# Attention with experts on one core: in the late steps three of 64 score tiles are exponentiated on VectorE, and expert rows are added six row tiles at a time

## The reference

```python
q = heads(x @ Wq.T); k = heads(x @ Wk.T); v = heads(x @ Wv.T)      # 16 heads of 8 columns
q = q * cos + _rotate_half_interleaved(q) * sin                    # k likewise
attn = jnp.einsum('bhnd,bhmd->bhnm', q, k) * scale
attn = jax.nn.softmax(attn, axis=-1)
out = jnp.einsum('bhnm,bhmd->bhnd', attn, v)
...
gate_weights = jax.nn.softmax(x @ gate_w + gate_b, axis=-1)
topk_vals, topk_idx = jax.lax.top_k(gate_weights, 2)               # 2 of 8 experts a row
h = gelu(x w1 + b1); h = gelu(h w2 + b2); expert_out = h w3 + b3
return jnp.sum(topk_vals[..., None] * gathered, axis=2)
```

## Time and profile before

| | us |
|---|---|
| three runs | 640.11, 642.52, 643.66 |
| median | 642.52 |
| the profiled execution | 641.5 |
| its span, first to last instruction | 639.8 |

### The profile page before, as it was taken

The page is one execution under the profiler, slowest core; times in us unless marked ns, Lnnn a source line. Parts: engine busy times, 40 slices in busy tenths (PEclk is TensorE's granted clock), DMA queues, the critical chain, the costliest instruction groups (busy, mean ns, idle before and its releaser), DMA issues.

```text
span 639.8 us, 12291 instructions
## 1 busy us (share of the span) xinstructions
PE 599.6 (94%) x4152; PEld 260.1 (41%) x4152; DVE 239.1 (37%) x742; ACT 546.8 (85%) x555; POOL 166.9 (26%) x187
## 2 busy tenths in 40 slices
PE   9889999999999998998999999999898998999895
PEld 6323332222222222222999999982222222222221
DVE  5655224766352335022565556630202020211204
ACT  3799999999999998999555555569999999999994
POOL 2700000001444444531122221223332333323310
PEclk9999999999999999999999999999999999999999
DMA  7654611532464246783333333311212111121204
GB/s 226 182 181 163 233 34 50 198 138 99 149 210 149 91 140 227 246 260 82 81 76 74 74 74 74 74 37 42 71 44 69 58 58 57 62 77 42 71 13 135
DMA packets 82625, 70.74 MB, mean 111 GB/s; under 512 B 44288, under 2 KB 58400, under 8 KB 82576
## 3 DMA queue, kind: packets, MB, share of 16 engines
q1 hardware_dynamic: 76000, 56.34, 29.1%
q0 software_dynamic: 5856, 13.05, 6.6%
q10 hardware_dynamic: 720, 0.71, 0.5%
HBM read 32.92 MB, written 32.96 MB: 103 GB/s over the span
## 4 chain that ended last, share of the span: by engine, by line
PE 62%; ACT 17%; issue 12%; DMA 3%; DVE 3%; SPq 1%; POOL 1%; DVEq 1%; ACTq 0%; POOLq 0%
PE ps L1411 18%; ACT probs L663 15%; PE ps L1394 11%; PE ps L1343 10%; PE ps L1335 5%; PE ps L1356 5%; PE ps L1318 3%; PE ps L1262 2%; ACT probs L641 2%; DMA k_st<-k_d 2%; DMA work<-slots_y_d,slot_i 2%; PE ps L1298 2%; PE ps L1225 1%; PE ps L1196 1%; DVE x_all L1133 1%
## 5 line engine op out<-in xcount | busy, mean ns | idle before, releaser
L663 ACT ACTIVATE probs<-ps 128x1536 f32<-128x1536 f32 (+1 forms) x308 | 408.6, 1432 | 8.2 <-PE ps L1394 6.6
L1411 PE MATMUL ps<-probs,v_st 128*32 128x512 f32 x1792 | 238.7, 604 | 4.4 <-DVE v_st L789 3.2
L1394 PE MATMUL ps<-q_st,k_st 32*128 32x512 f32 x896 | 154.5, 494 | 22.4 <-ACT probs L663 18.3
L1394 PEld LDWEIGHTS ps<-q_st,k_st 32*128 32x128 f32 x896 | 57.9, 181 | 235.0 <-ACT probs L663 172.7
L677 ACT ACTIVATE work<-ps,work 128x256 f32<-128x256 f32 (+1 forms) x156 | 64.9, 455 | 60.4 <-PE ps L1343 60.2
L541 POOL DMA_INDIRECT slots_x_d<-xn_all,slot_i x64 | 62.9, 983 | 196.9 <-DVE expert_i L987 127.2
L579 POOL DMA_INDIRECT work<-slots_y_d,slot_i x64 | 60.6, 947 | 122.0 <-PE ps L1411 79.2
L1343 PE MATMUL ps<-work 128*128 128x256 f32 (+1 forms) x312 | 68.0, 361 | 0.0
L641 ACT ACTIVATE probs<-ps 128x1024 f32<-128x1024 f32 x64 | 60.6, 1034 | 3.7 <-PE ps L1298 2.7
L1411 PEld LDWEIGHTS ps<-probs,v_st 128*32 128x32 f32 x1792 | 35.6, 107 | 60.7 <-issue 54.5
L789 DVE COPY v_st<-v_all 128x128 f32<-128x128 f32 (+1 forms) x32 | 8.5, 265 | 131.3 <-PE ps L1411 131.3
(11 more groups left out here) (177 smaller groups left out, 379.0 us busy)
## 6 DMA issues: line engine op xcount, KB each, us to landing
k_d<-parts SPq DMA_DIRECT2D x8, 1024.0 KB, 5.7
q_d<-parts SPq DMA_DIRECT2D x8, 1024.0 KB
q_st<-q_d SPq DMA_DIRECT2D x30, 256.0 KB
k_st<-k_d SPq DMA_DIRECT2D x30, 256.0 KB
slots_x_d<-parts SPq DMA_DIRECT2D x5, 1024.0 KB, 7.4
work<-slots_x_d SPq DMA_DIRECT2D x128, 32.0 KB, 1.9
slots_y_d<-work POOLq DMA_DIRECT2D x32, 128.0 KB, 2.2
work<-work SPq DMA_DIRECT2D x24, 128.0 KB
```

The source lines that it names most:

```text
L663: nc.scalar.activation(group_probs(phase, g)[:, 0:size, :], group_slot(g)[:, 0:size * HALF].rearrange("p (h n) -> p h n", n=HALF), ACT.Exp ...
L1394: ins = nc.tensor.matmul(group_slot(g)[:, n * HALF:(n + 1) * HALF], k_st[32 * h:32 * h + ROWS, mt * P:(mt + 1) * P], q_st[32 * h:32 * h + ...
L1411: ins = nc.tensor.matmul(o_ps[32 * h:32 * h + 32, :], v_window(mt, h, half), group_probs(phase, half * HALF_GROUPS + g)[:, n, :], start=be ...
```

## The change

In the late steps the 64 tiles of a step are dealt out anew (LATE_ITEMS). 60 go to ScalarE as 20 groups of three that run on across the two halves of the queries. The other four are one block, the second half of the queries with the first tile of keys. Their scores go one after another into aux_ps (help_scores, iterations 2 to 5). For heads 0, 3 and 2 VectorE reads them, scaled, into SBUF (read_help), and computes the exponential of all three at once, 1536 columns, by eight instructions (help_exps): split off the nearest power of two by adding a large constant, shift that into the exponent, evaluate a polynomial of fifth degree on the rest, multiply. Head 1 stays in aux_ps and is exponentiated by ScalarE after its group 7. The polynomial is not scaled to a leading coefficient of one; the factor that it lacks is put on ScalarE's exponentials too, as a bias of 6.62 (exp_bias), and falls out in the division. TensorE multiplies the helped block in iteration 17 (help_values). The turn of the last step's result moves from iteration 5 to 9, since aux_ps is in use before. A step has two groups fewer and is written as a loop of one step on TensorE and ScalarE; VectorE's late steps are written out.

Gathers are for six row tiles a step (GATHER = 6), in six steps instead of seven, paced by every second block, and added a step later, between the three readings of aux_ps. finish_rows for the first three batches moves to steps 11, 12 and 13. Steps before 9 are as before.

```diff
-GATHER = 5
+GATHER = 6
...
+LATE_ITEMS = [(0, mt, h) for mt in range(MT) for h in range(HG)] + [(1, mt, h) for mt in range(1, MT) for h in range(HG)]
+LATE_GROUPS = len(LATE_ITEMS) // 3
+LATE_BLOCKS = [(0, mt) for mt in range(MT)] + [(1, mt) for mt in range(1, MT)]
+HELP_AT = 2
+HELP_HEADS = (0, 3, 2, 1)
+HELP_VALUES = 17
+EXP_COEFFS = (-7.287735462188721, 41.80864715576172, -180.93753051757812, 522.0867309570312, -753.2122192382812)
+EXP_SHIFT = 6.62434696468868
+EXP_MAGIC = 1.5 * 2 ** 23 + 127 + 256
...
+        he_s, he_t, he_g, he_p = (part(2 * GATHER * C + 3 * HALF * k, 3 * HALF) for k in range(4))
...
+        help_probs = probs[:, PROB_RING - 1]
...
+                sp.wait_ge(S["scores_done"], group_units(t) + (LATE_ITEMS.index((0, MT - 1, HG - 1)) // 3 + 1))
                 load_half(q_st, q_d, t + 1, 0, S["q0_loaded"])
-                sp.wait_ge(S["scores_done"], group_units(t) + KEYS_READ)
+                sp.wait_ge(S["scores_done"], group_units(t) + (LATE_ITEMS.index((1, MT // 2 - 1, HG - 1)) // 3 + 1))
                 load_half(k_st, k_d, t + 1, 0, S["ka_loaded"])
-                sp.wait_ge(S["scores_done"], group_units(t) + GROUPS)
+                sp.wait_ge(S["scores_done"], group_units(t + 1))
...
-            for i in range(STEPS - SPLIT):
+            for i in range(STEPS - SPLIT - 1):
                 if i >= 1:
                     pool.wait_ge(S["combined"], i)
                 for k in range(min(GATHER, TILES - GATHER * i)):
-                    block_done((SPLIT + i) * BLOCKS + 3 * k)
+                    block_done((SPLIT + i) * BLOCKS + 3 + 2 * k)
...
+            def late_exps(t, first=False):
+                for g in range(LATE_GROUPS):
+                    act.wait_ge(S["scores_done"], group_units(t) + (g + 1))
+
+                    if g >= GROUP_RING:
+                        act.wait_ge(S["pv_done"], t * BLOCKS + (BLOCKS + late_sums((3 * (g - GROUP_RING) + 2) // HG)))
+                    elif first:
+                        act.wait_ge(S["pv_done"], t * BLOCKS + BLOCKS)
+                    else:
+                        act.wait_ge(S["pv_done"], t * BLOCKS + late_sums((3 * (g - GROUP_RING + LATE_GROUPS) + 2) // HG))
+                    nc.scalar.activation(late_probs(g), group_slot(g).rearrange("p (h n) -> p h n", n=HALF),
+                                         ACT.Exp, bias=exp_bias[:], scale=SCALE).then_inc(S["exp_done"], 1)
+                    if g == HELP_AT + 5:
+                        act.wait_ge(S["help_scored"], (t - SPLIT) * HG + HG)
+                        nc.scalar.activation(help_probs[:, 0, :], aux_ps, ACT.Exp, bias=exp_bias[:], scale=SCALE).then_inc(S["help_exp"], 1)
...
+            def combine(i, c):
+
+                tiles = range(GATHER * i, min(GATHER * i + GATHER, TILES))
+                dve.wait_ge(S["gathered"], 32 * tiles[-1] + 32)
+                if c:
+                    dve.wait_ge(S["comb_chain"], i + 1)
+                for k, tile in enumerate(tiles):
+                    ins = nc.vector.scalar_tensor_tensor(x_all[:, tile, :], gath[:, GATHER * c + k, :], gates[:, tile, c:c + 1], x_all[:, tile, :],
+                                                         ALU.mult, ALU.add)
+                ins.then_inc(S["combined" if c else "comb_chain"], 1)
...
+            def read_help(t):
+
+                for k in range(3):
+                    dve.wait_ge(S["help_scored"], (t - SPLIT) * HG + k + 1)
+                    nc.vector.tensor_scalar(he_s[:, k * HALF:(k + 1) * HALF], aux_ps, SCALE / math.log(2), None, ALU.mult)\
+                        .then_inc(S["help_read"], 1)
+                    if t > SPLIT and k < 2:
+                        combine(t - SPLIT - 1, k)
+
+            def help_exps(t, lo=0, hi=8):
+
+                for k in range(lo, hi):
+                    if k == 0:
+                        dve.wait_ge(S["help_read"], (t - SPLIT) * 3 + 3)
+                        ins = nc.vector.tensor_scalar(he_t, he_s, EXP_MAGIC, None, ALU.add)
+                    elif k == 1:
+                        ins = nc.vector.scalar_tensor_tensor(he_g, he_t, EXP_MAGIC, he_s, ALU.subtract, ALU.subtract)
+                    elif k == 2:
+                        ins = nc.vector.tensor_scalar(he_s.bitcast(I32), he_t.bitcast(I32), 23, None, ALU.logical_shift_left)
+                    elif k < 7:
+                        ins = nc.vector.scalar_tensor_tensor(he_p, he_g if k == 3 else he_p, EXP_COEFFS[k - 3], he_g, ALU.add, ALU.mult)
+                    else:
+                        nc.vector.scalar_tensor_tensor(help_probs[:, 1:HG, :].rearrange("p h n -> p (h n)"), he_p, EXP_COEFFS[4], he_s,
+                                                       ALU.add, ALU.mult).then_inc(S["help_made"], 1)
+                        return
+                    ins.then_inc(S["help_chain"], 1)
+                    dve.wait_ge(S["help_chain"], (t - SPLIT) * 7 + k + 1)
...
-            with dve.Fori(SPLIT, STEPS - 1) as t:
+            finished = {11: 0, 12: 1, 13: 2}
+            dve.wait_ge(S["x_scattered"], 16 * 2 * TILES)
+            for t in range(SPLIT, STEPS - 1):
+                read_help(t)
+                if t == SPLIT:
+                    for par in range(2):
+                        dve.wait_ge(y_stored[par], 16 * ((SLOT_TILES + 1 - par) // 2))
+                help_exps(t)
+                if t > SPLIT:
+                    normalise(t - 1)
+                if t in finished:
+                    dve.wait_ge(S["combined"], t - SPLIT)
+                    finish_rows(finished[t] * BT, BT).then_inc(S["out_ready"], 1)
                 load_v(t + 1, 0)
-                combine(t - SPLIT)
                 copy_o(t)
                 load_v(t + 1, 1)
-                normalise(t)
 
             last = STEPS - 1
+            read_help(last)
+            help_exps(last, 0, 4)
+            normalise(last - 1)
             copy_o(last, 0)
+            help_exps(last, 4)
             normalise(last, (0,))
-            combine(last - SPLIT, TILES - GATHER * (last - SPLIT))
-            dve.wait_ge(S["x_scattered"], 16 * 2 * TILES)
-            for b in range(B - 1):
-                finish_rows(b * BT, BT).then_inc(S["out_ready"], 1)
+            dve.wait_ge(S["combined"], last - SPLIT)
...
+            def help_scores(t, k):
+
+                if k == 0:
+                    pe.wait_ge(S["q1_loaded"], t * 16 + 16)
+                    free_aux(aux_of_turn(t - 1))
+                else:
+                    pe.wait_ge(S["help_read"], (t - SPLIT) * 3 + k)
+                h = HELP_HEADS[k]
+                nc.tensor.matmul(aux_ps, k_st[32 * h:32 * h + ROWS, 0:P], q_st[32 * h:32 * h + ROWS, HALF:N],
+                                 start=True, stop=True).then_inc(S["help_scored"], 1)
...
+            def help_values(t):
+
+                pe.wait_ge(S["help_exp"], t - (SPLIT - 1))
+                pe.wait_ge(S["help_made"], t - (SPLIT - 1))
+                for h in range(HG):
+                    ins = nc.tensor.matmul(o_ps[32 * h:32 * h + 32, :], v_window(0, h, 1), help_probs[:, (HELP_HEADS.index(h) + 1) % HG, :],
+                                           start=False, stop=False)
+                ins.then_inc(S["pv_done"], 1)
...
+                    if HELP_AT <= g < HELP_AT + HG:
+                        help_scores(t, g - HELP_AT)
+                    if g == HELP_AT + 7 and not first:
+                        turn(t - 1, 0, True)
+                    if g == 13 and last:
+                        turn(t, 0)
+                    if g == HELP_VALUES:
+                        help_values(t)
                     if g > 0:
...
```

More of the change, by code:

```diff
@@ L11 @@
+import math
 import concourse.bass as bass
@@ new lines, in late_scores @@
+            def late_scores(t, g, first=False):
+                items = LATE_ITEMS[3 * g:3 * g + 3]
+                if g == 0:
+                    pe.wait_ge(S["ka_loaded"], t * 16 + 16)
+                    pe.wait_ge(S["q0_loaded"], t * 16 + 16)
+                if (0, MT // 2, 0) in items:
+                    pe.wait_ge(S["kb_loaded"], t * 16 + 16)
+                if g >= 2 or not first:
+                    pe.wait_ge(S["exp_done"], group_units(t) + (g - 1))
+                for n, (half, mt, h) in enumerate(items):
+                    ins = nc.tensor.matmul(group_slot(g)[:, n * HALF:(n + 1) * HALF],
+                                           k_st[32 * h:32 * h + ROWS, mt * P:(mt + 1) * P],
+                                           q_st[32 * h:32 * h + ROWS, half * HALF:(half + 1) * HALF], start=True, stop=True)
+                ins.then_inc(S["scores_done"], 1)
```

126 lines of the change are left out of this document (70 added, 56 removed).

## The result

| | median us | runs | lowest to highest |
|---|---|---|---|
| before | 640.86 | 17 | 639.85 to 643.66 |
| changed | 643.41 | 17 | 642.35 to 646.27 |

The ratio is 1.0039 (95% interval 1.0026 to 1.0052). The change makes the kernel slower by 2.5 us; 632.5 was predicted, with 628.5 to 637.5 as the range. The sign was wrong.

A forecast was written before the change was run, and what follows sets the result against it. ScalarE was taken to bound the late steps. A gain of 12.6 less 0.7 (end stalls), 1.25 (help waits) and 1.1 (last step) is 9.5, giving 632.0 to 633.0 us; forecast 632.5, range 628.5 to 637.5.

The forecast's parts named there:

- ScalarE's part: Late steps: 20 three-tile activations and one of one tile take 27.1 us, not 28.9; 12.6 gained over seven.
- ScalarE pitch over 1.4 across many groups: Late steps: a sign named beforehand that would show the forecast wrong; 1.33 us was expected for three tiles.
- This is the whole gain that can be had: Late steps: ScalarE's pure pace gives 12.6 us over seven steps; the rest is what eats it.
- TensorE's part: Late steps: TensorE is not the bound on average; shrinking lead costs 0.1 us of stall per step, 0.7 in all.
- The wait of the third help score: Steps 10 to 14: it waits for VectorE's second read, stalling ScalarE 0.25 us each, 1.25 in all.
- rival A: Help reads slower than costed: 1.0 us stall in five steps instead of 0.25, about 636.5 us; chance 0.18.
- The polynomial: VectorE's eight instructions in late steps: 12.7 us, ending 21.0 into the step, hidden by ScalarE's work.
- The last step: Four polynomial instructions stand behind the first half's copy, help is 0.3 to 0.7 late; 1.1 us less gain.
- The gathers: Late steps: VectorE's wait of 3.9 us for gathered rows goes, with 2 in hand; it cost only a late copy_o.
- Rival C: VectorE's chain and POOL's gathers exclude each other, so the polynomial misses iteration 17: 656 us; chance 0.04.
- slower: Whole kernel: the outcome that the change makes it slower, given a chance of 0.04.

The follow-up runs named there:

- Experiment 1: The changed kernel with the bias of the late exponentials as the number 6.62 in the instruction instead of a column in SBUF: 632.30 us, ratio to before 0.9862.
- 2: The kernel before, with a column of zeros in SBUF as bias of the late exponentials instead of none: 652.08 us, ratio 1.0164.
- 3: The kernel before, with the late exponentials taking their scale from a column in SBUF instead of as a number, without bias: 652.36 us, ratio 1.0169.
- experiment 9: The kernel before with only the gather part: additions behind the division 653.28 us; ahead of it 639.67; ahead of it with gathers held back and bunched 639.60.
- experiments 4: The changed kernel with the bias as a number in even-numbered late groups, the column kept in odd ones and the one-tile activation: 640.62 us, ratio to before 1.0001.

## Why the prediction was wrong

**The step that failed** is "ScalarE's part", the first term of the sum. It took the pace of 1.33 for three tiles, and 0.49 for one, from rows of instructions that have no operand beside the tile in PSUM, and put it on instructions that have one. The diff shows `bias=exp_bias[:]`, and I read it as arithmetic that costs nothing. It costs 20 x 0.0925 + 0.08 = 1.93 a step, 13.5 over seven, more than the 12.6 that was to be gained. The prediction had named the sign itself, a "ScalarE pitch over 1.4 across many groups": it is 1.42 in all of them. "This is the whole gain that can be had" was right; it was spent in the same line.

The trace of before could have told. The gelus of the experts' layers take their bias from a column, and where two of 128 columns follow each other most closely their starts are 0.25 apart (306.85 and 307.10; a timeline that merges them):

```profile
306.85 0.62 ACT L677 ACTIVATE work<-ps,work 128x128 f32<-128x128 f32 x2
```

By the earlier trace rows 512 columns are 0.427, so 128 are 0.107 and 0.14 is the fixed part of a gelu; of an exponential it is 1.331 - 1.28 = 0.05. The difference is the 0.09. It was a hint and no proof, since a gelu is another function, of another shape. I never asked what the fixed part was.

The Trainium skill, "ScalarE: Activation LUTs", section "What ACT_TABLE_LOAD costs", states it outright: 186 ns + 0.833 N with scale and bias as immediates, and about 93 ns more for each [128,1] pointer operand. Experiments 1, 2 and 3 agree to the nanosecond or so (0.0925 for a bias, the same for a scale). I had read the page for what an exponential costs and had not held it against the changed call.

**What the rest of the sum was worth.** Experiment 1 is the kernel that I had priced: 632.3, where the sum had 632.0 for the profiled execution and I said 632.5. That is partly luck: the kernel before stood at 640.5 beside it, so the gain was 8.2 and not 9.5. Against the bare pace (27.1 a step) its steps have 4.7 us of pauses, where I had 0.7 + 1.25 + 1.1 = 3.05. The 12.6 was rounded early, 7 x 1.8; unrounded it is 202.62 - 7 x 27.1 = 12.9, and 12.9 - 4.7 = 8.2. (In the profiles it is 8.8 to the end of the span and 8.1 to the end of the last exponential; the stretch behind that varies by 0.8 between executions, from 7.35 to 8.18, in kernels of either kind.)

- TensorE's part: right in kind, too small in size. Pauses of 0.09 at the first two activations of steps 10 to 15 and of 0.06 to 0.14 at the last of steps 9 to 14 come to 1.6, where I had 0.7; no wait for q_st in the changed kernel.
- The wait of the third help score (and rival A with it): right in kind (its matmul starts at 493.32, 0.61 behind the scores at 492.71), too small in size: 0.48 in each of five steps with the number as bias, not 0.25. The delay itself, 0.6, was inside my 0.3 to 0.8, and six additions took 1.66, inside my 1.3 to 1.7; the lead was smaller than reckoned. In step 11 of experiment 1 the iteration with the first help score takes 1.60 (scores at 485.92 and 487.52) where I had 1.43, a help score "at nothing", so only some 0.12 of lead was there to give, not 0.31.
- The polynomial: right, 12.7 us and done 21.6 into a step. I had taken 0.04 between dependent instructions without a row for it; they stand 0.03 apart (12.72 less 2 x 0.96 and 6 x 1.76, over seven gaps).
- The last step: 0.77 of pauses in experiment 1 beside the usual two at the start, against 1.1 that I had put to the late help. The help makes 0.30 of it, and 0.47 are the wait for the copy of the first half, which I had not named.
- The gathers: right. "It costs nothing today but a late copy_o": 1.3 us in experiment 9, of which the 0.7 in pauses was part of the 12.6.
- Rival C: its meeting is real, and POOL pays for it. Of the 64 gathers of the changed kernel the 41 that overlap a VectorE instruction of 0.9 us or more take 1.02 to 2.31 us, and the 23 others 0.94 or 0.95. VectorE's instructions keep their 1.76. In 34 of the 41 the gather ends 0.81 or 0.82 behind the end of the VectorE instruction that ran when it started, whether that has one tensor or two (the gather of 499.64 ends at 501.82, the instruction at 501.01). In six the next one is L1213, with one tensor, and the gather ends 0.12 behind that; a next one with two tensors holds nothing up. Since the last gather of a step still lands before the additions ask, nobody pays.

```profile
499.64 2.18 POOL L614 DMA_INDIRECT work<-slots_y_d,slot_i  x1 [0.30 <-issue]
...
512.62 0.94 POOL L614 DMA_INDIRECT work<-slots_y_d,slot_i  x1 [0.30 <-issue]
```

**13.5 lost, 9.5 to be won, yet only 2.5 slower.** The slower pace gave some of the waits back. At 1.42 a group TensorE keeps up in iterations with values (1.43), so the pauses of 0.1 are gone and the one at the help is 0.27 to 0.33 instead of 0.48; all pauses together are 1.6 instead of 4.7. So 13.5 + 1.6 - 12.6 = 2.5 (2.2 with the unrounded 12.9).

What I would have had to write as a rival was a fifth: the gain is right and the new form of the instruction eats it. The 0.04 that I gave to "slower" all went to a late polynomial.

## What to carry to other kernels

When a diff changes the form of the instruction that sets the pace (one more operand, another type, another memory), price that form before anything else, from rows that have it, and do not take the row that has the same shape. A constant belongs into the instruction as a number: a column in SBUF costs ScalarE 0.09 us each time, 7% of a 1536-column exponential. And a slower engine hides waits: what an edit beside it is worth (some 0.7 us for the order of the reads) can be larger once the pace is back (1.8).

## What the runs showed of the hardware

- A [128,1] operand of an activation, bias or scale, puts its successor off by 0.0925 us; a number as bias costs nothing; the cost is of the single instruction (experiments 1 to 4).
- A gather issued by POOL stretches from 0.94 to a median of 1.49 and at most 2.3 us beside VectorE's fp32 instructions over 1536 columns in SBUF, those with one tensor as well as with two (1.63 to 1.64 where L1209, with one, runs at its start); VectorE isn't slowed. The scatter of the earlier trace rows beside an instruction of 0.68 was not.
- Signals of TensorE can come 1.2 to 2.7 us after the start of their matmul instead of 0.52, at the same place of step after step, while TensorE's own rows look undisturbed (experiments 4 and 9). Some of these signals have no record at all (before has 338 of 372 for its scores), so only those count for which ScalarE waited. The cause was not found.
